# ScalarE's table sets chosen by the functions ahead, and the order of steps replaced, in a two-layer network on one core

## The chip, the cores and the metric

One core of one Trainium2 chip runs the whole kernel. The metric is device microseconds (us) of that core, the median of several runs. The kernel before took 1077.08 us (three runs: 1076.49, 1077.08, 1081.83).

## The reference

The input x is 4 sequences of 1024 rows of 128 values, 4096 rows in fp32. Four residual steps follow each other, each on a layer norm of x:

```python
x = x + attention(layernorm(x))     # 16 heads of width 8, softmax over 1024 keys, inner residual and layer norm
x = x + ffn(layernorm(x))           # silu(x W1) * (x W2), gelu (512x512), gelu (512x512), down to 128
x = x + gla(layernorm(x))           # gated linear attention, 8 heads, a recurrence over 1024 steps per sequence
x = x + zones(layernorm(x))         # per sequence a router picks 3 of 8 experts: gelu_tanh(x Wa) Wb, weighted
```

## The kernel before, in words

The 4096 rows are 8 blocks of 512 (`b` 0 to 7; a sequence is two blocks). The work is cut into 13 streams of steps, each a Python generator in the class `Plan`: `x` attention scores, their exponentials and the weighing of values; `q` the query, key and value projections of the next block; `a` what follows attention; `b` the FFN; `p` projections and decay of the gated linear attention; `r` its replicated value rows (a DMA each); `s` its recurrence, as 128 products, scans and queries; `t` its norm, gate and output, and the router; `w`, `f`, `l`, `z` loads; `d` the experts. The constant `ORDER` is a string of 1805 letters; `Plan.rest` takes the next step of the stream that each letter names. The result is one list of steps (`order`), and each engine's program is that same list, cut down to the steps in which the engine has a part. So the order on every engine and every DMA queue is fixed by that string, each engine works strictly in order, and semaphores are waited on where data come from another engine.

Steps that the text below speaks of:

- `scores` and `weigh` (stream `x`): 256 `scores` steps; in each, TensorE makes two score tiles of 128 x 1024 (4 matmuls, L1448) and ScalarE takes the exponential of both (L914, 512 in all). `weigh`, 512 of them, multiplies an exponentiated tile with the values (L1485). From the seventh of 32 head pairs on, two PSUM areas hold scores, so scores of one step wait for the exponentials of the step before.
- `gate` (L925), `level` with `gelu` (L930), `down`: the FFN of a block. `gate_mm` and `hid_mm` on TensorE are L1517. TensorE works there on a value's high and low part; the low part is made by VectorE (L1222) or, for some, by GpSimd (`parts`, L848).
- `flag` (stream `q`, one per block): GpSimd's PARTITION_ALL_REDUCE (L838), of which block 0's comes at the start. In the order before, block 2's and block 4's stand ahead of a low part of the FFN that TensorE needs next; after, such a part stands just ahead of them. Low parts on GpSimd stand close behind those of blocks 5, 6 and 7 in the order after, queries close behind those of blocks 3 and 4.
- `decay_1`, `decay_3`: Exp (L949), Ln (L951) and Exp (L958). `rms`: Ln (L1003) and then Exp (L1005). `tanh_c` Tanh (L1010), `route_1` Tanh (L1019), `route_2` Exp (L1024).
- `product` and `state` (L1252, L1261) on VectorE and `query` (L862) on GpSimd: the recurrence, 128 times.
- `zone_up` (TensorE L1632, ScalarE L1038) and `zone_down` (TensorE L1644): the experts, 96 each. They start when the last scores are done, since they reuse the attention's memory.

ScalarE's table is loaded by `tables(name)` (L877 to L881; the load itself is an instruction at L881), called ahead of each looked-up function. The rule before: anything with Exp or Ln asks for the set that has both; Gelu and the approximated Gelu ask for a set each; Tanh is content with either Gelu set and else loads the Gelu set. A load is issued only if the set asked for isn't the loaded one. Since the list of steps is known when the program is written, so is each load.

Of the kernel before, what the change touches and what calls it, by code (L numbers as in the profile page):

```python
# [22 lines left out]

ORDER = (
    "xxxxxwxxxxxxqxqxqxxlxxxxxxxxwxxwqxxxxxxxxwxwxxxxxqxxwxxqwxxxfxxxxfxxlxxlxxxxxwxxwxxwxlxwxfxxqfwaxwxx"
    "xxxwxxxxxxxxxwxaawwxxxwaxwwxxqxxwxlafxxxxxxxxxaqxxwxxaxxxwfxbxxwxqbxbbxqbxxfxxbxbbxxxxxlbbxxbqlbbbbb"
    "xbqlxbbbbxbxxxxbfxpxbxbxxppxxxarparxxprpapxxxxxxxssrxasalxraxxxxqxaxxpsssxqbxxsbbxbxxrsqsxxxxsxssssx"
    "xxxxsqxxbsxbbxssbxqxrxxxrxssxlxsxrxsrbssxslxflqsxfsfbbxbxsbbxsbbbsxsfxbrrxxsbrassbbsxsrbxbxsssxaxxsx"
    "axxsxsxssxbrxaxbxaxaxqpxrxpalrxsqpsxsxssrxbxspxppxxqxssssxspxsxsrbxbbbbxxsssfxrxbxrqbxqsxfbxxrsxxbbs"  # L30
    "bssssstbbsxxsbxxxxxxrbrrtsssxxxbbstsllsbxsftblbsrxsxxbxxxbfqsxaxxssxsrsbrxxxxxxxarxxxsfsasxtrxxxsxsx"
    "xxassxsbxslsssxrxpqsrpxxxsqrxsrsxtatpxpsxxxxfaxsxpxxqtqxxxpssasxxspxqxxxxsblqxxtbsbsxbbbtbblrbsrxxxx"
    "xrfstssrslxsxssbsxtstxbbstbbsbbsxbxtbrbrxfrssstxssxbsbsxtasxsbrxbxsassaxxxxxbxsaraxrtsssbxxaxrfsxptp"
    "xsrxsxsxxsxastxsqxbtxqxxtsspsrrqxbsbsxbsxrsxsxxxpxlfrxbqspbpssxsxxpsxbsbxxsxsqxrlssxrqxsbrsxrxxsssxt"
    "xxxxlxxsttlxxsbxfbsxsbbbsbbfxbsrxxtxbbsxrrxsssssrsbssbssssxtratxbsxxbxsxxrsxxssasbaxbxrrlxpxxxxsxxps"
    "txsssxsasaxxfxrtxxsraxsfxrxqxxaxpxqrsbpsxxxsxxtxpxpsxxqssxqbxsxsxqsxxbxlbptxblbbbxssxxrxbxrxslxxstxs"
    "tbssbbsrbsbxsrxtsbsffxssxbxsbtxxrtssrbxsbbssabsrxrxsbsxxbxtxxsxsbtxstxssrxssfsxrxxxaatrxrxsbxppxssxt"
    "xslsxxxsxxassaxxpstsrxxxsrpsxfsxxxrxssrxsxppxasssxtxsaxpxsssxtrxxtrxsrsrsssxbssxtxxxxxtfztsbbfbzbbsb"
    "bdsbdadtssbzbbbsraaddbbbbsdartszdtdsssbsbdarrbsdsssbdabsdssdrdbdadtzbssdrsdrstdddbtdsbddsrddssspssds"
    "zdsrbbtddspsdrdbdrspdsddpbsdbppdsrdbbsssptddbssdssrdrdsbstsbbdsrbdssdssbtsdbrdbstdbssdtsdrsrssrbssbt"  # L40
    "brbssdsssbbtssdtsdbrdrdssrsddbstsssdsrsssdppddstsdrdptdrrsdssdtdsrdddpsspdddtptsststsdpsdssrrssddddd"
    "sdtdsrzsssssdtrsstsdtsrzddsrssdtddsdddsdrssrtsdstsszdsdsrsrsrsssdsrdddddsddsssssdddsrssddtsdddrssddt"
    "ddssdsdtddtddddttddddttddtddtddddtdttdtdtttzdzdddddzdddddddddddddddddddddddddddddddddddddddddddddddd"
    "ddddd"
)

# [427 lines left out]
def build(nc, io, out):  # L474
    ctx = ExitStack()
    with ctx:
# [8 lines left out]
        order = plan.order  # L485
# [386 lines left out]
        def _(act):  # L872
            need = Waits(act, S)
            own = Chain(need, "act")
            loaded = [None]

            def tables(name):  # L877

                if loaded[0] != name:
                    loaded[0] = name  # L880
                    act.preload_act_table_set(name)  # L881

            def log_exp():
# [61 lines left out]

            def decay_1(b):
                own.settle()
                log_exp()
                own.step(act.activation(G2, G2, ACT.Exp, scale=-1.0))  # L949
                own.settle()  # L950
                act.activation(G2, G2, ACT.Ln, bias=1.0).then_inc(S["g_abs"], 1)  # L951

            def decay_3(b):
                need.wait_ge("decayed", 2 * b + 1)
                if b:
                    need.wait_ge("scanned", 16 * b)
                log_exp()
# [74 lines left out]
            def zone_up(b, n, bk, e):  # L1032
                t = 12 * b + n
                need.wait_ge("zone_up_ps", t + 1)
                if t >= NH:
                    need.wait_ge("zone_mm", t - NH + 1)
                tables("gelu_apprx_tanh_and_others")
                act.activation(HH[t % NH], bank(bk), ACT.Gelu_apprx_tanh).then_inc(S["hidden"], 1)  # L1038

            def zone_down(b, m, bk):  # L1040
                if m or b % 2:
                    return
                for n in range(3 * (b // 2), 3 * (b // 2) + 3):
# [662 lines left out]
```

## Time and profile before

| | |
|---|---|
| median of three runs | 1077.08 us (1076.49 to 1081.83) |
| the profiled execution | 1080.35 us, its span 1078.6 us |
| TensorE busy | 978.0 us, 91% |
| ScalarE busy | 846.4 us, 78%; of it 512 exponentials of 128 x 1024 486.8 us, 108 table loads 138.6 us |
| VectorE busy | 707.4 us, 66% |
| GpSimd busy | 343.3 us, 32% |
| mean granted TensorE clock | 0.973 of 2.4 GHz |

The span runs from the first to the last instruction of the core; the 1.75 us between it and the execution's time lie outside. A TensorE matmul's end is modelled, so a busy TensorE need not be at its peak pace. The attention's exponentials run from 26.2 to 794.5 us; what is left of the other streams, and the experts, come after.

### The profile page before, as it was taken

What the parts mean: (1) busy time and instruction counts of PE and PEld (TensorE: products, weight loads), DVE (VectorE), ACT (ScalarE), POOL (GpSimd) and SP (SyncE); (2) the same over time, 40 slices, a digit from 0 to 9 for tenths busy, and PEclk for the clock granted to TensorE, in tenths of its full rate; (3) what the DMA queues carried; (4) which work ended last, traced back from release to release, by engine and by line L of the source; (5) the groups of instructions that cost most, each with busy time, mean ns of one, the idle gap of its engine ahead of it and who ended that gap; (6) DMA issues with size and microseconds to landing.
All of it is one profiled execution on the core that took longest, in us unless ns stands there. A gap on an engine that the chain in (4) does not pass through costs nothing.

```text
span 1078.6 us, 16699 instructions
## 1 busy us (share of the span) xinstructions
PE 978.0 (91%) x5842; PEld 462.2 (43%) x5842; DVE 707.4 (66%) x1267; ACT 846.4 (78%) x1082; POOL 343.3 (32%) x318
## 2 busy tenths in 40 slices
PE   2998989998898799989989999899889999999998
PEld 1222336222442343334423443354237667655666
DVE  4234652565577556878896696778787888989200
ACT  0998996998797799989999989999977377653542
POOL 1000111112442332434522542334332655646100
PEclk8899999899898899999999999999999999999999
DMA  6755352225504361473136431631332321242020
GB/s 165 183 137 126 96 139 57 76 65 131 129 30 126 90 133 57 108 181 95 45 102 162 116 88 61 180 96 55 104 105 73 98 67 62 91 130 83 11 69 20
DMA packets 139975, 106.27 MB, mean 99 GB/s; under 512 B 91824, under 2 KB 106960, under 8 KB 139856
## 3 DMA queue, kind: packets, MB, share of 16 engines
q1 hardware_dynamic: 134960, 102.77, 35.4%
q10 hardware_dynamic: 4896, 1.87, 0.7%
q8 instruction: 79, 1.29, 0.5%
q14 instruction: 40, 0.33, 0.1%
HBM read 75.25 MB, written 29.36 MB: 97 GB/s over the span
## 4 chain that ended last, share of the span: by engine, by line
PE 51%; ACT 17%; issue 14%; DVE 9%; DMA 5%; POOL 4%; SPq 1%; ACTq 0%; DVEq 0%; POOLq 0%
PE PS L1485 15%; ACT R L914 10%; PE PS L1517 9%; PE PS L1448 9%; PE PS L1632 4%; PE PS L1644 4%; DMA R<-VD 3%; DVE R L1252 3%; PE PS L1557 2%; ACT L881 2%; DVE R L1261 2%; PE PS L1579 2%; POOL R L862 2%; PE PS L1588 1%; PE PS L1383 1%
## 5 line engine op out<-in xcount | busy, mean ns | idle before, releaser
L914 ACT ACTIVATE R<-PS 128x1024 f32<-128x1024 f32 x512 | 486.8, 1038 | 52.7 <-PE PS L1448 50.8
L1485 PE MATMUL PS<-R 128*32 128x512 f32 x2048 | 294.0, 617 | 0.2 <-DVE R L1205 0.2
L862 POOL TENSOR_TENSOR R<-R 128x512 f32<-128x512 f32 x128 | 182.2, 1430 | 175.0 <-ACT R L989 121.6
L1448 PE MATMUL PS<-RA 32*128 32x512 f32 x1024 | 189.2, 506 | 46.4 <-ACT R L914 30.5
L1517 PE MATMUL PS<-RB,WR 128*128 128x512 f32 x640 | 183.5, 430 | 24.6 <-DVE R L1228 10.2
L1261 DVE TENSOR_TENSOR_SCAN R<-R 128x512 f32<-128x512 f32 x128 | 192.5, 1504 | 2.9
L1448 PEld LDWEIGHTS PS<-RA 32*128 32x128 f32 x1024 | 73.7, 185 | 273.2 <-ACT R L914 168.6
L881 ACT ACT_TABLE_LOAD x108 | 138.6, 1283 | 48.7 <-PE PS L1517 23.2
L1517 PEld LDWEIGHTS PS<-RB,WR 128*128 128x128 f32 x640 | 121.1, 196 | 86.8 <-issue 22.4
L1252 DVE TENSOR_TENSOR R<-R 128x512 f32<-128x512 f32 x128 | 108.2, 845 | 28.6 <-DMA R<-VD 28.5
L1038 ACT ACTIVATE R<-PS 128x512 f32<-128x512 f32 x96 | 56.6, 596 | 77.1 <-PE PS L1632 76.6
L848 POOL TENSOR_TENSOR RB<-R,RB 128x512 fp32r<-128x512 f32 x48 | 69.6, 1451 | 146.6 <-DVE RB L1217 125.3
L1644 PEld LDWEIGHTS PS<-R 128*128 128x128 f32 x768 | 97.4, 191 | 39.3 <-issue 37.0
L1644 PE MATMUL PS<-R 128*128 128x128 f32 x768 | 100.1, 276 | 2.9 <-ACT R L1047 2.8
L1632 PE MATMUL PS<-XT,R 128*128 128x512 f32 x192 | 99.0, 607 | 2.4 <-DMA R<-in_Wb 2.1
L821 POOL TENSOR_SCALAR rs<-mv 128x4 f32<-128x4 f32 x40 | 15.5, 387 | 248.2 <-DVE mv L1077 230.3
L1485 PEld LDWEIGHTS PS<-R 128*32 128x32 f32 x2048 | 46.9, 109 | 90.7 <-issue 77.4
L1217 DVE CAST RB<-R 128x512 fp32r<-128x512 f32 x64 | 33.9, 530 | 42.2 <-ACT R L930 41.6
L1205 DVE COPY R<-PS 128x512 f32<-128x512 f32 x32 | 22.0, 687 | 59.8 <-PE PS L1485 59.7
L930 ACT ACTIVATE R<-PS,sB 128x512 f32<-128x512 f32 x64 | 42.0, 687 | 11.4 <-PE PS L1517 10.9
L823 POOL TENSOR_TENSOR rs<-rs,half 128x4 f32<-128x4 f32 x40 | 49.1, 1227 | 3.3
L1588 PE MATMUL PS<-R,hot 128*32 128x512 f32 x256 | 42.4, 602 | 5.8 <-POOL R L862 5.1
(123 smaller groups left out, 844.9 us busy)
## 6 DMA issues: line engine op xcount, KB each, us to landing
R<-VD SPq DMA_DIRECT2D x128, 256.0 KB
RA<-QD SPq DMA_DIRECT2D x64, 256.0 KB, 4.5
QD<-RA SPq DMA_DIRECT2D x56, 256.0 KB, 4.0
RA<-QD SPq DMA_DIRECT2D x64, 128.0 KB, 4.4
OD<-R SPq DMA_DIRECT2D x32, 256.0 KB, 2.1
R<-OD SPq DMA_DIRECT2D x128, 32.0 KB, 2.5
R<-in_Wa SPq DMA_DIRECT2D x12, 256.0 KB, 3.3
R<-in_Wb SPq DMA_DIRECT2D x12, 256.0 KB, 3.9
```

Of the source, the lines that this page charges most:

```text
L848: pool.tensor_tensor(part(tile(dst)[:, 1, :]), whole(src), part(tile(dst)[:, 0, :]), ALU.subtract).then_inc(S["lo_pool"], 1)
L862: pool.tensor_tensor(st, st, Qc, ALU.mult).then_inc(S["qh"], 1)
L881: act.preload_act_table_set(name)
L914: act.activation(PR[u % 4], bank(2 * s, 1024), ACT.Exp, scale=SC).then_inc(S["exp"], 1)
L1038: act.activation(HH[t % NH], bank(bk), ACT.Gelu_apprx_tanh).then_inc(S["hidden"], 1)
L1252: dve.tensor_tensor(ST[n % NS], ST[n % NS], Kc, ALU.mult).then_inc(S["kv"], 1)
L1261: dve.tensor_tensor_scan(st, Ac, st, CS[:, v:v + 1] if k else 0.0, ALU.mult, ALU.add).then_inc(S["scanned"], 1)
L1448: op = pe.matmul(bank(2 * s + h), exact(KS[k][p:p + 32, 128 * j:128 * j + 128]), exact(QS[k][p:p + 32, :]), start=True, stop=stop)
L1485: op = pe.matmul(bank(ob)[c:c + 32, :], VAF[b % 2][:, at:at + 32], PR[u % 4][:, 512 * h:512 * h + 512], start=(j == 0), stop=(j == 7), til ...
L1517: return pe.matmul(out_ap, w, x, **kw)
L1632: pe.matmul(bank(bk), WA[r][:, 128 * m:128 * m + 128], xtblock(b), start=True, stop=True).then_inc(S["zone_up_ps"], 1)
L1644: op = pe.matmul(bank(bk)[:, 128 * i:128 * i + 128], HH[t % NH][:, 128 * i:128 * i + 128], WB[r][:, m % 4, :], start=(m == 0 and i == 0), ...
```

## The change

Two things change, nothing else.

1. ScalarE's `tables` takes the function (exp, ln, tanh, gelu, the approximated gelu) and no longer a set. It knows the whole list of functions to come. If the loaded set has the function, nothing is loaded.
2. The string `ORDER` is another one. It has the same letters, each as often, in another order.

```diff
 ORDER = (
-    "xxxxxwxxxxxxqxqxqxxlxxxxxxxxwxxwqxxxxxxxxwxwxxxxxqxxwxxqwxxxfxxxxfxxlxxlxxxxxwxxwxxwxlxwxfxxqfwaxwxx"
+    "qxqxqxxxxxxxxxxxxxwxlxxwxwxxqxwxxxxxxxxxxxwxxxxxxqfxxxxxwxxwxxxlxfxwwxxqxxxxlxqxwxxxxwlxxxxpxfxxxwwf"
...
-            loaded = [None]
-
-            def tables(name):
-
-                if loaded[0] != name:
-                    loaded[0] = name
-                    act.preload_act_table_set(name)
-
-            def log_exp():
-                tables("natural_log_exp_and_others")
-
-            def tanh_with(name):
-                if loaded[0] not in ("gelu_and_others", "gelu_apprx_tanh_and_others"):
-                    tables(name)
+            EXP, LOG, GELU, APPR = "exp_and_others", "natural_log_exp_and_others", "gelu_and_others", "gelu_apprx_tanh_and_others"
+            sets = {"exp": (EXP, LOG), "ln": (LOG,), "tanh": (EXP, GELU, APPR), "gelu": (GELU,), "appr": (APPR,)}
+            uses = {"scores": ("exp",), "gate": ("tanh",), "gelu": ("gelu",), "decay_1": ("exp", "ln"), "decay_3": ("exp",),
+                    "rms": ("ln", "exp"), "tanh_c": ("tanh",), "route_1": ("tanh",), "route_2": ("exp",), "zone_up": ("appr",)}
+            coming = ["exp"] + [f for step in order for f in uses.get(step[0], ())]
+            state = {"loaded": None, "at": 0}
+
+            def tables(function):
+
+                at = state["at"]
+                assert coming[at] == function
+                state["at"] += 1
+                if state["loaded"] not in sets[function]:
+                    def run(name):
+                        return next((n for n in range(at, len(coming)) if name not in sets[coming[n]]), len(coming))
+                    state["loaded"] = max(sets[function], key=run)
+                    act.preload_act_table_set(state["loaded"])
...
             def decay_1(b):
                 own.settle()
-                log_exp()
+                tables("exp")
                 own.step(act.activation(G2, G2, ACT.Exp, scale=-1.0))
                 own.settle()
+                tables("ln")
                 act.activation(G2, G2, ACT.Ln, bias=1.0).then_inc(S["g_abs"], 1)
...
             def rms(b, bk):
                 need.wait_ge("mean_ps", b + 1)
-                log_exp()
+                tables("ln")
                 act.activation(T1, bank(bk), ACT.Ln, scale=1.0 / 16.0, bias=epsc[:, 0:1]).then_inc(S["rms"], 1)
                 need.wait_ge("rms", b + 1)
+                tables("exp")
                 act.activation(T1, T1, ACT.Exp, scale=-0.5).then_inc(S["inv_rms"], 1)
```

The other callers change one word each (`log_exp()` to `tables("exp")`, `tanh_with(...)` to `tables("tanh")`, the two Gelus to `tables("gelu")` and `tables("appr")`).

Walking the list of steps with each rule, as the program text does, gives the loads that are issued (the one at the start included):

| | loads up to the last `scores` step | after it | in all |
|---|---|---|---|
| order before, rule before | 75 | 33 | 108 |
| order after, rule after | 58 | 25 | 83 |

Of the 83, 29 are for Gelu, 11 for the approximated Gelu, 16 bring the set with Ln (8 of them for `rms`, 4 for `decay_1`, 4 for `scores`) and 27 the set with Exp and Tanh. By the same walk the order before with the rule after would issue 87, and the order after with the rule before 140.

Up to head pair 16 (of 32) of the attention the walk counts, without the load at the start, 33 loads before and 23 after.

What lies ahead of the last `scores` step differs by little else: after the change it holds 28 `gate` steps in place of 24 (with the 16 matmuls of L1517 that belong to them), 4 more splittings into parts, one `product` less and one `query` less. The first `hid_mm` of block 6 stands just behind that step. At the very start, the norm of block 1 (`stats`, `apply`) and its four transposes (`turn_in`) now stand around the first `scores` step instead of after the sixth.

## Rows read from the trace of the kernel before

**Rows 1.** The page: busy time, share of the span, instructions of two engines.
```profile
PE 978.0 (91%) x5842; PEld 462.2 (43%) x5842; DVE 707.4 (66%) x1267; ACT 846.4 (78%) x1082; POOL 343.3 (32%) x318
```

**Rows 2.** Busy time by stretch: start:end, length, then each engine.
```profile
26.00:150.00 124.00, 117.36 (x772) 34.13 (x766) 56.01 (x127) 114.19 (x123) 7.31 (x10) 0.96 0.52 131
150.00:415.00 265.00, 237.75 (x1410) 104.99 (x1408) 152.05 (x297) 218.57 (x259) 73.57 (x71) 0.94 0.38 96
415.00:794.50 379.50, 349.63 (x2232) 141.29 (x2230) 298.08 (x526) 355.06 (x449) 145.58 (x132) 1.00 0.39 105
794.50:1078.60 284.10, 265.78 (x1394) 177.53 (x1392) 190.68 (x280) 157.04 (x251) 111.97 (x89) 0.99 0.24 73
```

**Rows 3.** The same stretches for the table loads alone (L881).
```profile
150.00:415.00 265.00, 41.06 (x32) 0.94 0.38 96
415.00:794.50 379.50, 51.32 (x40) 1.00 0.39 105
794.50:1078.60 284.10, 42.34 (x33) 0.99 0.24 73
```

**Rows 4.** Who waited for whom, 415 to 794.5 us: total, times, longest.
```profile
PEld PS L1448 <- ACT R L914: 98.7, 147, 1.7
ACT R L914 <- PE PS L1448: 12.0, 29, 1.8
```

**Rows 5.** The same, 150 to 415 us.
```profile
PEld PS L1448 <- ACT R L914: 58.4, 82, 1.9
ACT R L914 <- PE PS L1448: 16.5, 23, 3.2
ACT L881 <- PE PS L1517: 13.4, 5, 5.5
PE PS L1517 <- POOL RB L848: 7.8, 4, 4.4
```

**Rows 6.** Groups of instructions by line, the whole span.
```profile
L914 ACT ACTIVATE R<-PS 128x1024 f32<-128x1024 f32 x512 | 486.8, 1038 | 52.7 <-PE PS L1448 50.8
L881 ACT ACT_TABLE_LOAD x108 | 138.6, 1283 | 48.7 <-PE PS L1517 23.2 <-issue 11.6 <-PE PS L1632 5.8
L925 ACT ACTIVATE R<-PS,sB 128x512 f32<-128x512 f32 x32 | 21.7, 686 | 15.5 <-PE PS L1517 15.3
```

**Rows 7.** ScalarE in order of time: start, length, instruction.
```profile
400.56 1.94 ACT L914 ACTIVATE R<-PS 128x1024 f32<-128x1024 f32 x2
402.52 1.28 ACT L881 ACT_TABLE_LOAD   x1
403.82 0.60 ACT L1010 ACTIVATE R<-PS 128x512 f32<-128x512 f32 x1
...
524.06 3.77 ACT L914 ACTIVATE R<-PS 128x1024 f32<-128x1024 f32 x4 [0.48 <-PE PS L1448]
```

**Rows 8.** The start, in order of time.
```profile
7.59 1.11 PE L1369 MATMUL PS<-ident,R 128*128 128x128 f32 x4 [7.59 <-DVE R L1086]
...
26.19 3.77 ACT L914 ACTIVATE R<-PS 128x1024 f32<-128x1024 f32 x4 [13.05 <-PE PS L1448]
26.45 1.12 DVE L1086 TENSOR_SCALAR R<-X,mv,rs 128x128 f32<-128x128 f32 x4 [5.80 <-POOL rs L823]
```

**Rows 9.** Around two of GpSimd's reductions, in order of time.
```profile
173.26 2.50 POOL L848 TENSOR_TENSOR RB<-R,RB 128x512 fp32r<-128x512 f32 x2 [7.30 <-issue]
...
365.26 0.37 POOL L838 PARTITION_ALL_REDUCE R<-R  x1 [5.92 <-issue]
...
372.60 1.25 POOL L848 TENSOR_TENSOR RB<-R,RB 128x512 fp32r<-128x512 f32 x1 [6.97 <-issue]
...
373.90 5.70 PE L1517 MATMUL PS<-RB,WR 128*128 128x512 f32 x17 [4.38 <-POOL RB L848]
374.72 1.28 ACT L881 ACT_TABLE_LOAD   x1 [5.46 <-PE PS L1517]
```

**Rows 10.** The chain of waits that ended last, 794.5 to 1078.6 us, by line.
```profile
by line: PE PS L1632 14.7%; PE PS L1644 14.4%; DMA R<-VD 12.9%; DVE R L1252 8.4%; DVE R L1261 7.9%; issue 7.7%; POOL R L862 4.3%; PE PS L1517 3.9%; PE PS L1588 2.6%; DMA R<-in_Wb 1.7%; ACT L881 1.7%; PE PS L1557 1.3%; POOL rs L823 1.1%; SPq
```

More of the change, by code:

```diff
@@ L31 @@
[L31 to L40, printed above, removed]
@@ L41 @@
[L41 to L43 removed]
+    "qxqxqxxxxxxxxxxxxxwxlxxwxwxxqxwxxxxxxxxxxxwxxxxxxqfxxxxxwxxwxxxlxfxwwxxqxxxxlxqxwxxxxwlxxxxpxfxxxwwf"
+    "wxxwxxaxxxwxwxxaawxxxawaqxxwxlxxxxaxxxxxqxwxawxfxxbwxxxxxwxqxxxbxxbbxxbbxbqxxxbbxlqxxbxxbbbbbbxblxxb"
@@ new lines @@
+    "xxlfbfbbxxbxxxqfxxxbxxxxxaaxbxxabxxaxplpxxrrrxpqaqpxpxapqqxfxpxaxxsxxxxbxsxbxsxxsqsxxsxssrxxxssbxqxx"
+    "rxxxlssxbxrssfxbxfbxlxssssbrxxbbrsxxsxxxlxxsxsrxsrsbsxbxbbbfbbxbxssxabssbxssrsrssbsrsbsxxrbbxxsaasxs"
+    "xbxxxsbaxxpssxpsxaxqrsxsrasxxxqssrlxfppxrabqxxxpsxpxsssxspxxxbxsssxxxxxbrqxxrbxbxbxrbxbxbssqsxstxbts"
+    "rbstssxsxbsbsqbbbxxssxxxxrsbststlxrxxfrbllxbbrssxbssxssfsbxsbxxfaxxxxbssrxaaxxrsrxxsxssxxxsrbsxaxpsx"
+    "xpssxxsssxqasxrrxxxxsxsxqxrsprsaqxtxlxtxspxxaxqxpsxbpsxssxspsxxbxxxftqssxbxbrbrrxxbxxxxxqsblsslrxxbb"
@@ new lines @@
+    "sxxlstfsxxsbssxtssbsbsrbxfbbbtxbssxrxbbsxfssbsrsaxbssarssstxbxaxbtxaxtxxxxsbrxxatrxxsxxxtsxsbasrxxsx"
+    "fsssasxtrspxqslxxbpssrxrxrqbqspxqtxxbstbxpsxsqsbxtxxxxsxppttssxsrxxlbxpxssxssxxbxrbsxrrxrsssxxsxslxs"
+    "sxtsssttbxxsfsrlxxtxfxsfsqbbbbbtxbxrbxsxbssxtbsbrxsbssbxxxtarssbxbxaxxasxxasbrraslxxaxrsxxxxsbxsssxs"
+    "qpsxxpsxrxxtxspxsqasxsprxxxbsxsxxrsxrfrssxsqxpxpxsxfqsxsxpxxstbsxxsxsxtxqbrlxbxxbxbrbxsxrbxrlsxlxbtx"
+    "sssxssbssbxfxbbbbbfbssxxxstsxbrxrtxarsssxbssrsbssstsbxbxxbtxxxabxssasxrtrxbxrsssrxsppsxxsxsxxsxxasxx"
@@ new lines @@
+    "xxpxxsstsftsrpaxxxxsssxrxarssxxtsrxapbpsssxsltxpxxxfsbsxsxtrbbbrxxbrxsbrxsbssxtxxsfxbxxtxxtsssbxszbf"
+    "btbbtstsbssbdrbadtbbabassbdazzasbbdatrrsdsddtdsdsrdtddbadbbssssdsdsrbprstdsdbddsdrdbpdsddbdddrzdtsbs"
+    "dszsdsbtsbdsbzdsdpsprtdsdsdrbsssrpbspdssrsdbsbpsbssrbsbddbtrsssdrdddsrdsdssstssdtsbsrttrbsdrssssbdbr"
+    "ssdsdsbddbsttsssdbdrdrssdsbrdrsstsssdppsddpsssdsddprdstrddddtdssstdspdrstrdtddpsstssdsptssrsrdddtdss"
+    "srdsddztsrsssddtsdtssdzstrsssrsdddrddsrtsdsssddtsdsdssrsrszssdrdsrdsddsddsdtdsssdsddsddrssdsdrdssdsd"
@@ L44 @@
+    "dsdtdsdtddtdddtdtddtddttdddddtdddtdttdtttzztdzdddddddddddddddddddddddddddddddddddddddddddddddddddddd"
     "ddddd"
@@ L923, in gate @@
                     need.wait_ge(*free)
-                tanh_with("gelu_and_others")
+                tables("tanh")
                 act.activation(HL[0][m][:, 1, :], bank(ba), ACT.Tanh, scale=sB[:, m:m + 1]).then_inc(S["tanh"], 1)
@@ L928, in gelu @@
                 need.wait_ge(*ps)
-                tables("gelu_and_others")
+                tables("gelu")
                 act.activation(HL[L][m][:, 1, :], bank(bk), ACT.Gelu, scale=sB[:, scale + m:scale + m + 1]).then_inc(S["gelu"], 1)
@@ L947, in decay_1 @@
                 own.settle()
-                log_exp()
+                tables("exp")
                 own.step(act.activation(G2, G2, ACT.Exp, scale=-1.0))
                 own.settle()
+                tables("ln")
                 act.activation(G2, G2, ACT.Ln, bias=1.0).then_inc(S["g_abs"], 1)
@@ L956, in decay_3 @@
                     need.wait_ge("scanned", 16 * b)
-                log_exp()
+                tables("exp")
                 act.activation(Ac, G1, ACT.Exp, scale=1.0 / 16.0).then_inc(S["decayed"], 1)
@@ L1001, in rms @@
                 need.wait_ge("mean_ps", b + 1)
-                log_exp()
+                tables("ln")
                 act.activation(T1, bank(bk), ACT.Ln, scale=1.0 / 16.0, bias=epsc[:, 0:1]).then_inc(S["rms"], 1)
                 need.wait_ge("rms", b + 1)
+                tables("exp")
                 act.activation(T1, T1, ACT.Exp, scale=-0.5).then_inc(S["inv_rms"], 1)
@@ L1008, in tanh_c @@
                 need.wait_ge(*ps)
-                tanh_with("gelu_and_others")
+                tables("tanh")
                 act.activation(Z1, bank(bk), ACT.Tanh, scale=0.5).then_inc(S["tanh_c"], 1)
@@ L1017, in route_1 @@
                 need.wait_ge("route_ps", 2 * bt + 1)
-                tanh_with("gelu_and_others")
+                tables("tanh")
                 act.activation(router[0:32, bt, 2:3], bank(bk)[0:32, 0:1], ACT.Tanh, bias=b1r[:, 0:1]).then_inc(S["route_act"], 1)
@@ L1022, in route_2 @@
                 need.wait_ge("logits_r", bt + 1)
-                log_exp()
+                tables("exp")
                 act.activation(router[:, bt, 16:24], router[:, bt, 8:16], ACT.Exp).then_inc(S["route_act"], 1)
@@ L1036, in zone_up @@
                     need.wait_ge("zone_mm", t - NH + 1)
-                tables("gelu_apprx_tanh_and_others")
+                tables("appr")
                 act.activation(HH[t % NH], bank(bk), ACT.Gelu_apprx_tanh).then_inc(S["hidden"], 1)
```

4 lines of the change are left out of this document (removed).

## The prediction

> **What bounds the kernel now.** I read the page's first part, then busy time by stretch, then the chain and the waits. The page puts TensorE first, 91%, and ScalarE at 78% [rows 1]. That average hides two stages. Up to 794.5 us the 512 exponentials run, and there ScalarE is busy 92% (26 to 150), 82% (150 to 415) and 94% of the stretch (355.06 of 379.50); behind them it falls to 55%, with TensorE at 94% [rows 2]. TensorE's 92% in the third stretch is pipelined matmuls with modelled ends, so busy time doesn't say who sets the pace; the waits do. From 415 to 794.5 us TensorE's weight loads of the scores wait 98.7 us in 147 places for an exponential, while ScalarE waits 12.0 us for scores [rows 4]. So there **ScalarE sets the pace**. Between 150 and 415 us it is less plain: ScalarE has 46 us idle in 265 [rows 2], waiting 16.5 us for scores and 13.4 us, in 5 places of up to 5.5 us, for the FFN's products, some of these held up by GpSimd (7.8 us) [rows 5]; the granted clock is 0.94 against 1.00 later [rows 2], nearer the upper of its two levels (2.4 GHz, the other 1.2) in both.
>
> After 794.5 us the chain is mixed: the experts' two matmul lines 29%, the recurrence (replica DMA, product, scan, query) 12.9 + 8.4 + 7.9 + 4.3 = 33.5%, table loads 1.7% [rows 10].
>
> **The change, part by part.** The profiled execution took 1080.35 us with a span of 1078.6, 3.3 us above the median of 1077.08; I sum differences and take them from the median.
>
> *Table loads ahead of the last scores: 75 become 58, 17 fewer.* The walk gives 75 before, and the trace has 33 of 108 behind 794.5 us [rows 3], so the walk and the trace agree. A load lasts 1283 ns, each one [rows 6]. What it takes from ScalarE is a little more. Two exponentials start at 400.56 and last 1.94, the load starts at 402.52, the next activation at 403.82 [rows 7]: gaps of 0.02 and 0.02 us. Without a load two activations overlap: four exponentials take 3.77 us, 0.94 each, against 1.94/2 = 0.97 in a group of two [rows 7] and 1.04 for one [rows 6], so neighbours overlap by some 0.1 us, which a load between them forbids. 0.02 + 1.28 + 0.02 + 0.08 = **1.40 us a load**. 17 x 1.40 = **-23.8 us**, on the path where ScalarE sets the pace. Ten of the 17 fall before pair 16 (up to about 400 us), where it is the pace only in part; I let them count in full, because there too TensorE's weight loads wait for exponentials in 82 places, 58.4 us, more than three times what ScalarE waits for scores [rows 5], and keep 10 x 1.40 = 14 us for the range.
>
> The Trainium skill, "ScalarE: Activation LUTs", section What ACT_TABLE_LOAD costs, puts a drain of about 1.38 us on top of the 1283 ns, 2.66 us for a switch; this trace agrees with the 1283 and shows no such gap on either side [rows 7]; by the page 17 loads would be 45 us. The same page's rules for kernel authors speak against splitting Exp and Ln over sets (the joint set is one load, not two). Here the new rule does pay for it.
>
> Ln now forces a load where Exp's set is in: 8 loads for `rms` and 4 for `decay_1` among the 83. They are in the counts already, so no term of their own. They stand in chains with little behind them at once; if one lands on the path, 1.40 us.
>
> *Table loads behind the last scores: 33 become 25, 8 fewer.* ScalarE is busy 157 of 284 us [rows 2], so TensorE's work and the recurrence cover them: **0**. With the cover gone, -8 x 1.40 = -11 us; that end goes into the range.
>
> *Work pulled ahead of the last scores.* Four `gate` steps more: 4 x 0.686 [rows 6] = **+2.7 us** on ScalarE. Sixteen matmuls of L1517 leave the tail. The nearest row has 17 in 5.70 us [rows 9], 0.34 each, so up to 5.4 us of TensorE. A third of the tail's chain is the recurrence [rows 10], which gets one product more, so I take **-3** of the bounds 0 and -5.4.
>
> *The start.* The four transposes of block 1 now stand on TensorE between the first and second `scores`, and wait for a norm that ends at 26.45 + 1.12 = 27.57 us; transposes at the cold start took 1.11 us [rows 8]. So the second scores start at about 28.7 and their first exponential at about 29.5, where before four exponentials ran on from 26.19 [rows 8], the third at 28.1: **+1.5 us**, between 0 and +3.
>
> *GpSimd's reductions.* Behind each of the eight PARTITION_ALL_REDUCE GpSimd stands still for 7.0 to 7.3 us [rows 9]. Before, one of them falls between the gates' third and fourth low part, so that TensorE waits 4.38 us and ScalarE 5.46 us for it [rows 9]. In the new order the block's fourth low part stands ahead of the reduction at both such places (blocks 2 and 4), but pooled parts follow others closely. I take half of the 4.4: **-2 us**, bounds -8 (all of the 7.8 us [rows 5]) and +8 (the same again somewhere else).
>
> *The rest of the order.* The same instructions and DMAs on each queue, in another order; SP's queue carries the same transfers. Nothing in the trace prices the new interleaving: bounds -8 and +8, from the 7.8 us that TensorE waits for one kind of GpSimd's work [rows 5], taken at 0.
>
> Sum: -23.8 + 2.7 - 3 + 1.5 - 2 = **-24.6 us**, so 1077.1 - 24.6 = **1052.5 us**.
>
> **The rivals.**
>
> *Rival 1, TensorE keeps the pace.* If up to 415 us the freed ScalarE time only becomes idle time, 14 us come back: 1066.5. If that holds later as well, nothing is left but small terms: 1077. For it: TensorE's 91%, and its 90% against ScalarE's 82% from 150 to 415 [rows 2]. Against: the 98.7 us of waits on the exponentials [rows 4]. Chance 0.17, half of it above 1071.7.
>
> *Rival 2, slower, a GpSimd hole behind the reductions.* The new order puts a pooled low part within one or two scores steps behind the reduction in blocks 5, 6 and 7, and queries behind those of blocks 3 and 4. If TensorE, which works in order, reaches the consumer within the 7.2 us, the scores behind it wait too and ScalarE runs dry. Seven reductions at 7.2 us are 50; less the 7.8 us paid before [rows 5] that is +43, and with -22.6 from the other terms +20: 1097. It decides from an average stall of (22.6 + 7.8)/7 = 4.3 us a reduction. Against: between such a part and its consumer lie mostly other gates and scores. Chance 0.06.
>
> *Rival 3, a load costs its surroundings too.* ScalarE idled 48.7 us just before the 108 loads [rows 6], 0.45 each. If that goes with the load, and the tail counts: 25 x (1.28 + 0.45) = 43.3, with the other terms' -0.8 that is 1033. By the Trainium skill's 2.66 us (the same page and section) the 25 would be an estimated 66.5 us, 1010. Against both: 11.6 of the 48.7 is the start, and most of the rest waits for products that come no sooner. Chance 0.05.
>
> *Rival 4, the change doesn't do what it says.* If the set with Exp doesn't serve Tanh, and loads are put in after all, the new order comes near its 140 loads under the old rule: 32 x 1.40 = +45, 1122. Chance 0.02.
>
> **How the numbers follow.** Forecast 0.70, rivals 0.17, 0.06, 0.05, 0.02. 0.5%, about what a measurement of this kernel can tell from no change, is 5.4 us: faster means below 1071.7. Faster: 0.68 of the forecast, 0.09 of rival 1, 0.05 of rival 3: 0.82. Same: 0.02 of the forecast's own upper end and 0.08 of rival 1: 0.10. Slower: rivals 2 and 4, 0.08. The forecast's own range: down to 1040 with the tail's loads or the stalls gone, up to 1066 with rival 1's 14 us. To hold 8 in 10 it reaches on to 1074, through most of rival 1.
>
> **What would show it.** Right: 83 loads, 58 before the last exponential; ScalarE's busy time down by 25 x 1.28 = 32 us to about 814; the exponentials' end, 794.5 now, at about 794.5 - 23.8 + 2.7 + 1.5 - 2 = 773; the tail 281 us instead of 284 [rows 2]; the second pair of exponentials about 1.5 us later. Wrong: as many loads gone but ScalarE's idle time before 415 us grown by 10 us or more (rival 1); TensorE waiting on L848 or L862 by over 20 us (rival 2); the last exponential before 755 (rival 3); more than 83 loads (rival 4). The forecast fails as a whole if the stretch up to the last exponential shrinks by less than 12 us.

## The result, and the profile after

The changed kernel takes 1045.09 us (four runs, 1042.45 to 1051.1) against 1077.63 us for the kernel before, a ratio of 0.970 with a 95% interval of 0.965 to 0.975: **32.5 us faster**. The forecast was 1052.5 us, 24.6 us faster, in a range of 1040 to 1074. The profiled execution took 1046.05 us, its span 1044.2.

The page's busy times:

```profile
PE 962.5 (92%) x5842; PEld 454.1 (43%) x5842; DVE 720.2 (69%) x1267; ACT 813.4 (78%) x1057; POOL 359.4 (34%) x318
```

Busy time by stretch (start:end, length, then TensorE, its weight loads, VectorE, ScalarE, GpSimd, granted clock, DMA share, GB/s); the last exponential ends at 772.9 us here:

```profile
26.00:150.00 124.00, 120.62 (x833) 37.57 (x830) 61.96 (x142) 116.03 (x126) 10.62 (x13) 0.97 0.54 137
150.00:415.00 265.00, 242.56 (x1487) 102.69 (x1485) 166.42 (x312) 226.07 (x273) 79.52 (x74) 0.96 0.38 99
415.00:773.00 358.00, 335.27 (x2116) 136.68 (x2112) 297.42 (x508) 325.17 (x418) 156.88 (x131) 0.99 0.41 107
773.00:1044.20 271.20, 256.54 (x1374) 173.16 (x1372) 183.95 (x268) 144.56 (x239) 107.37 (x85) 0.99 0.25 76
```

They answer to [rows 2]. ScalarE's busy time is 813.4 us, where 814 was foretold, and the exponentials end at 772.9, where 773 was. The tail behind them is 271.3 us against 284.1 and against 281 in the forecast. So the sum missed in the tail, by 10 us, and seems to have hit the attention's part to a tenth. The experiments show that this second hit was luck in good part: taken apart in the kernel before, neither of its two large terms is what the sum had.

The table loads by stretch (they answer to [rows 3]): 83 in all, 25 behind the exponentials.

```profile
150.00:415.00 265.00, 33.36 (x26) 0.96 0.38 99
415.00:773.00 358.00, 39.77 (x31) 0.99 0.41 107
773.00:1044.20 271.20, 32.08 (x25) 0.99 0.25 76
```

Who waited for whom in the changed kernel (total, times, longest), TensorE from 26 to 772.9 us, and below it ScalarE:

```profile
PE PS L1453 <- ACT R L917: 17.3, 52, 0.7
PE PS L1593 <- POOL R L862: 7.5, 4, 4.4
PE PS L1522 <- POOL RB L848: 5.0, 2, 4.0
...
ACT R L917 <- PE PS L1453: 62.3, 64, 13.1
ACT L891 <- PE PS L1522: 9.6, 5, 5.4
ACT R L968 <- POOL R L862: 5.2, 1, 5.2
```

L1453, L1522, L1593 and L917 are L1448, L1517, L1588 and L914 of before. Against the kernel before, over the same part, TensorE waits less for exponentials and less for low parts:

```profile
PE PS L1448 <- ACT R L914: 30.5, 79, 2.1
...
PE PS L1517 <- POOL RB L848: 9.6, 6, 4.4
```

but a wait for GpSimd's queries (L862), which wasn't there over this part, has come in. It is looked at below.

### The profile page after: what moved, and what is told of

Read it like the earlier page. It is cut to its first block, busy times and chain, and to the rows that moved or that the text cites. A ratio compares the mean times of both kernels' runs of the same rounds, so it can differ in the third digit from the quotient of the medians.

```text
span 1044.2 us, 16674 instructions
## 1 busy us (share of the span) xinstructions
PE 962.5 (92%) x5842; PEld 454.1 (43%) x5842; DVE 720.2 (69%) x1267; ACT 813.4 (78%) x1057; POOL 359.4 (34%) x318
## 4 chain that ended last, share of the span: by engine, by line
PE 56%; issue 14%; ACT 12%; DVE 10%; POOL 4%; DMA 3%; SPq 0%; DVEq 0%; ACTq 0%; POOLq 0%
PE PS L1490 17%; PE PS L1453 10%; PE PS L1522 9%; ACT R L917 8%; PE PS L1649 5%; PE PS L1637 5%; DVE R L1266 3%; PE PS L1562 3%; PE PS L1584 2%; DMA R<-VD 2%; DVE R L1257 2%; POOL R L862 2%; PE PS L1593 2%; PE PS L1388 1%; ACT L891 1%
## 5 line engine op out<-in xcount | busy, mean ns | idle before, releaser
L917 ACT ACTIVATE R<-PS 128x1024 f32<-128x1024 f32 x512 | 489.0, 1037 | 65.4 <-PE PS L1453 62.3
L862 POOL TENSOR_TENSOR R<-R 128x512 f32<-128x512 f32 x128 | 196.3, 1542 | 180.1 <-ACT R L993 108.2
L1453 PE MATMUL PS<-RA 32*128 32x512 f32 x1024 | 176.8, 501 | 34.1 <-ACT R L917 17.3
L1266 DVE TENSOR_TENSOR_SCAN R<-R 128x512 f32<-128x512 f32 x128 | 199.8, 1561 | 3.2
L1522 PE MATMUL PS<-RB,WR 128*128 128x512 f32 x640 | 177.8, 420 | 12.0 <-POOL RB L848 5.0
L1453 PEld LDWEIGHTS PS<-RA 32*128 32x128 f32 x1024 | 68.6, 183 | 251.6 <-ACT R L917 154.7
L1522 PEld LDWEIGHTS PS<-RB,WR 128*128 128x128 f32 x640 | 117.7, 192 | 80.3 <-issue 35.3
L1257 DVE TENSOR_TENSOR R<-R 128x512 f32<-128x512 f32 x128 | 112.3, 878 | 35.1 <-DMA R<-VD 33.9
L1649 PEld LDWEIGHTS PS<-R 128*128 128x128 f32 x768 | 98.7, 193 | 39.1 <-issue 38.0
L1490 PEld LDWEIGHTS PS<-R 128*32 128x32 f32 x2048 | 46.9, 109 | 95.4 <-issue 82.2
L1593 PE MATMUL PS<-R,hot 128*32 128x512 f32 x256 | 49.3, 616 | 10.7 <-POOL R L862 10.7
L823 POOL TENSOR_TENSOR rs<-rs,half 128x4 f32<-128x4 f32 x40 | 46.5, 1162 | 3.3
L1343 DVE TENSOR_TENSOR X<-PS,X 128x512 f32<-128x512 f32 x8 | 5.5, 685 | 52.4 <-PE PS L1649 52.4
```

The lines of the kernel that those rows point to most:

```text
L862: pool.tensor_tensor(st, st, Qc, ALU.mult).then_inc(S["qh"], 1)
L1257: dve.tensor_tensor(ST[n % NS], ST[n % NS], Kc, ALU.mult).then_inc(S["kv"], 1)
L1266: dve.tensor_tensor_scan(st, Ac, st, CS[:, v:v + 1] if k else 0.0, ALU.mult, ALU.add).then_inc(S["scanned"], 1)
L1453: op = pe.matmul(bank(2 * s + h), exact(KS[k][p:p + 32, 128 * j:128 * j + 128]), exact(QS[k][p:p + 32, :]), start=True, stop=stop)
L1490: op = pe.matmul(bank(ob)[c:c + 32, :], VAF[b % 2][:, at:at + 32], PR[u % 4][:, 512 * h:512 * h + 512], start=(j == 0), stop=(j == 7), til ...
L1522: return pe.matmul(out_ap, w, x, **kw)
```

## The experiments

All ratios are to the kernel before, timed on the same chip. "Attention" is from the first exponential to the end of the last, "tail" from there to the end of the span, both in the profiled execution. Single executions scatter: three that run the same instructions (changed, e3_tail2, e4_att2) have attentions of 746.7, 751.0 and 745.7 us and tails of 271.3, 272.1 and 270.6. The profiled execution of before lies 3 us above its median, that of e2_order 4 us below.

| run | loads | attention, us | tail, us | median, us | ratio (95%) |
|---|---|---|---|---|---|
| before | 108 | 768.3 | 284.1 | 1077.6 | 1 |
| changed | 83 | 746.7 | 271.3 | 1045.1 | 0.970 (0.965 to 0.975) |
| e1_rule | 87 | 761.5 | 284.4 | 1073.6 | 0.996 (0.993 to 0.999) |
| e2_order | 140 | 815.7 | 272.9 | 1120.9 | 1.043 (1.037 to 1.049) |
| e5_more | 146 | 811.2 | 282.2 | 1122.7 | 1.045 (1.039 to 1.051) |
| e6_tail20 | 103 | 749.5 | 278.1 | 1053.4 | 0.978 (0.972 to 0.985) |
| e7_new40 | 40 | 745.9 | 268.6 | 1043.1 | 0.970 (0.964 to 0.977) |
| e8_early_zone | 84 | 747.3 | 283.2 | 1058.4 | 0.986 (0.979 to 0.993) |
| e9_old40 | 40 | 767.4 | 283.4 | 1082.8 | 1.006 (1.003 to 1.008) |
| e10_old_nored | 87 | 755.7 | 276.9 | 1062.9 | 0.987 (0.982 to 0.992) |
| e11_new_nored | 83 | 720.8 | 271.6 | 1023.1 | 0.950 (0.947 to 0.953) |
| e12_banks | 83 | 746.8 | 270.2 | 1044.8 | 0.970 (0.965 to 0.976) |

### e1_rule and e2_order: the change cut in two

e1_rule is the changed kernel with the old string, e2_order the kernel before with the new one:

```diff
 ORDER = (
-    "qxqxqxxxxxxxxxxxxxwxlxxwxwxxqxwxxxx...
+    "xxxxxwxxxxxxqxqxqxxlxxxxxxxxwxxwqxxx...
```

> The rule of the change with the order of before: 87 loads, 55 up to the last scores (20 fewer than before) and 32 behind it (1 fewer). Theory A (a load costs 1.40 us up to the last scores and nothing behind it, as the prediction has it): 1077.6 - 20 x 1.40 = about 1050 us, the exponentials end at 794.5 - 28 = 766, the tail stays at 284. Theory B (a load costs as much behind the last scores): 1048, not to be told from A here. Theory C (the tail's 12.8 us in the changed kernel came from the new order): the tail keeps its 284 us here, and the order is worth what is left, some 5 us. Rival (TensorE sets the pace up to 415 us, so that only the loads after that pay): some 1063.

> The order of the change with the rule of before: 140 loads, 115 up to the last scores (57 more than the changed kernel) and 25 behind it (as many). Theory A: 1045.1 + 57 x 1.40 = 1125 us, all of it before the exponentials' end, the tail 271 us as in the changed kernel. If only the loads where ScalarE sets the pace count, half of that: about 1085.

The rule alone makes the kernel 0.4% faster, not 2.6%. Twenty loads fewer shorten the attention by 6.8 us, 0.34 us a load in place of 1.40. That is little more than single executions scatter, but the interval of the ratio, 0.993 to 0.999, is far from theory A's 2.6%. The order alone makes the kernel 4.3% slower, 1120.9 us where theory A had 1125: by this run alone theory A would have stood. The two together are worth far more than their sum. The stretch from 26 us to the end of the exponentials, for before, e1_rule, the changed kernel and e2_order, in that order:

```profile
26.00:794.50 768.50, 704.74 (x4410) 280.42 (x4404) 506.14 (x949) 687.82 (x829) 226.46 (x212) 0.97 0.40 106
```
```profile
26.00:787.60 761.60, 698.63 (x4410) 277.36 (x4404) 501.12 (x947) 662.45 (x809) 227.20 (x212) 0.97 0.40 107
```
```profile
26.00:772.90 746.90, 698.36 (x4429) 276.90 (x4426) 525.70 (x961) 667.27 (x815) 246.91 (x217) 0.98 0.42 109
```
```profile
26.00:842.00 816.00, 732.97 (x4423) 283.40 (x4420) 523.28 (x962) 744.41 (x872) 239.48 (x217) 0.93 0.38 100
```

In e1_rule ScalarE works 25.4 us less than before (687.82 - 662.45) and the stretch is 6.9 us shorter: 18.5 us turned into idle time, and TensorE idles 63.0 us against 63.8. That is the mechanism of rival 1, though the new order hid it. The step from e1_rule to the changed kernel has TensorE as busy (698.4) and ScalarE a little busier, and is 14.7 us shorter: it is TensorE's idle time that fell, from 63.0 to 48.5 us. In e2_order the 57 loads more than in the changed kernel cost 69.0 us of attention, 1.21 us each (75.8 us of the whole by the medians, 1.33 each); ScalarE is busy 91% of it. Part of that price is TensorE's own: its granted clock is 0.93 there against 0.98 and its busy time 34.6 us longer.

How the attention's gain splits therefore depends on which half comes first: with the rule first it is 6.8 us and then 14.8 for the order; with the order first it is 47.4 us lost and then 69.0 won. The run that would tell most, the new order with 75 loads up to the last scores like the kernel before, wasn't made. On a straight line between the changed kernel and e2_order it would lie an estimated 17 x 1.21 = 20.6 us above the changed kernel, within 1 us of the kernel before. So it isn't shown that the new interleaving is faster at an equal number of loads; what is shown is that with 58 or fewer of them it is.

The tail is plainer: 284.4 us with the old order and the new rule, 272.9 with the new order and the old rule. The tail's 12.8 us come from the order, theory C; the order by itself also takes the tail's loads from 33 to 25 (the trace of e2_order has 25 there).

### e5_more, e7_new40 and e9_old40: loads put in and taken out

e5_more is the kernel before with 38 loads put in:

```diff
                 if loaded[0] != name:
                     loaded[0] = name
+                    if name == "gelu_and_others" and state["early"]:
+                        act.preload_act_table_set("gelu_apprx_tanh_and_others")
                     act.preload_act_table_set(name)
```

> The kernel before with 38 loads more up to the last scores: each load of the Gelu set there is preceded by one of the other Gelu set (146 in all). Theory D (new: an order of steps hides little of a load that it wasn't made for, and gives little back for one that is taken out of it, 0.34 us each in the order before): 38 x 1.3 = 49 us slower than before, 1129. If loads in the order before are mostly covered anyway (the 0.34 us of the rule alone holds both ways): 13 us, 1093.

e7_new40 is the changed kernel with Tanh in place of the FFN's 64 exact Gelus, so that part of the computation is left out and another of the same cost stands there; e9_old40 is the same with the old order:

```diff
-                tables("gelu")
-                act.activation(HL[L][m][:, 1, :], bank(bk), ACT.Gelu, scale=sB[:, scale + m:scale + m + 1]).then_inc(S["gelu"], 1)
+                tables("tanh")
+                act.activation(HL[L][m][:, 1, :], bank(bk), ACT.Tanh, scale=sB[:, scale + m:scale + m + 1]).then_inc(S["gelu"], 1)
```

> The changed kernel with Tanh computed in place of the FFN's 64 exact Gelus (same cost of an activation, so 40 loads in all: 21 up to the last scores in place of 58, 19 behind). Theory A (each load pays 1.3 to 1.4 us wherever ScalarE sets the pace): 1045 - 37 x 1.35 = 995 us. Theory D (taken out of an order that was made with them, they give about 0.34 us each): 1045 - 13 = 1032 us, and ScalarE's idle time up to the exponentials' end grows from 80 to about 115 us.

> The order of before with the new rule and with Tanh computed in place of the FFN's 64 exact Gelus (40 loads, 21 up to the last scores, 19 behind). Theory E (new: TensorE with its fixed interleaving sets the pace once ScalarE is relieved, and the new order lowers that floor): the exponentials end near 787, as with 55 loads, and the time is within 4 us of the 1073.6 of the rule alone, some 28 us above the changed kernel although it has 43 loads fewer. Theory A (loads pay wherever they are taken out): 1073.6 - 34 x 1.35 = 1028 us.

Each load put into the old order costs 1.13 us of attention (42.9 us over 38), 1.25 of the whole by the medians of the runs made together (1122.7 - 1075.2 = 47.5 over 38). But taking 37 out of the attention's part of the changed kernel gives 0.8 us there, 0.02 us a load and less than the scatter, and taking 54 of 75 out of the old order's gives 0.9 us, less than taking 20 out had. The rows of e7_new40, same columns as above, and of its loads:

```profile
26.00:772.20 746.20, 699.82 (x4429) 277.26 (x4426) 527.29 (x961) 620.31 (x778) 246.64 (x217) 0.97 0.42 109
```
```profile
L891 ACT ACT_TABLE_LOAD x40 | 51.3, 1283 | 24.2 <-issue 11.6 <-DVE R L1266 8.0 <-PE PS L1601 2.7
```

ScalarE works 47.0 us less than in the changed kernel (667.27 - 620.31), and the stretch is 0.7 us shorter. TensorE's busy time is the same to 1.5 us, and its waits for exponentials stay too (16.0 us in 50 places, in the changed kernel 17.3 in 52). **Once ScalarE isn't overloaded, its work doesn't set the pace any more; the order of the steps does.** That the pace is then TensorE's, with what it waits for in that order, is argued from its 94% busy and not shown; GpSimd's share in it follows below. The two orders have different floors: 761 to 767 us of attention for the old one with 55 or 21 loads up to the last scores, 746 for the new one with 58 or 21. With its 75 the kernel before stood 1 to 7 us above its floor; the new order's 58 stand on it. So the price of a load is not one number but has a kink: 1.1 to 1.3 us above what the order has room for, nearly nothing below. Theory A is out. Theory D had the price of a load put in (1129 us, 1122.7 measured) but not of one taken out (1032, 1043.1 measured), and theory E holds in kind, though e9_old40 took 1082.8 us where it had 1073.6 within 4.

e9_old40 is even 0.9% slower than e1_rule (intervals 1.003 to 1.008 and 0.993 to 0.999), with 47 loads fewer. TensorE is 5.2 us longer busy and idle 1 us longer there, at a clock of 0.96 against 0.97 (behind 415 us 0.96 against 0.99); the cause stays open.

### e3_tail2 and e4_att2: loads issued twice

Both put a second `act.preload_act_table_set(state["loaded"])` behind the first, e3_tail2 behind the last scores, e4_att2 up to them.

> The changed kernel with each of the 25 loads behind the last scores issued twice. Theory A (covered): within 3 us of 1045. Theory B (the tail's loads are on the path, so that 8 fewer gave 11 of the 12.8 us): 1045 + 25 x 1.3 = 1078 us. In between, the cost per load times 8 is what the loads gave the tail.

> The changed kernel with each of the 58 loads up to the last scores issued twice (the first one stands in ScalarE's idle start, 57 count). Theory A: a second load adds 1.30 us (1.28 and a gap of 0.02; the overlap was lost to the first): 57 x 1.30 = 74, so 1119 us. Rival (TensorE or bubbles cover part of them): 1080 to 1100, with ScalarE's idle time before the exponentials' end falling from about 57 us.

Neither tells anything: the second load of a set that is in was dropped, and the trace of each has 83 loads. So they are two more measurements of the changed kernel: 1046.29 us (0.970) and 1043.21 us (0.969). e5_more and e6_tail20 therefore put in loads of another set.

### e6_tail20: do the tail's loads count?

```diff
+                own_sets = sets if at <= 366 else {"exp": (LOG,), "ln": (LOG,), "tanh": (EXP,), "gelu": (GELU,), "appr": (APPR,)}
-                if state["loaded"] not in sets[function]:
+                if state["loaded"] not in own_sets[function]:
```

> The changed kernel with 20 more loads behind the last scores (45 in place of 25; Exp and Ln only from their joint set, Tanh only from Exp's set there), 103 in all. Theory A (covered there): within 3 us of 1045, the tail 271. Theory B (on the path): 20 x 1.3 = 26 us, 1071. The 8 fewer loads of the change gave the tail 8/20 of what this costs.

Between the two theories: 20 loads make the tail 6.8 us longer, 278.1 against 271.3, 0.34 us each, and the whole by the medians 8.3 us, 0.42 each. By that the 8 that went were worth an estimated 3 us where the prediction had 0.

### e8_early_zone: the tail's opening

The letters of the changed order behind the last scores; three steps of the experts move ahead of the FFN's:

```diff
-    szbfbtbbtstsbssbdrbadtbbabassbdazz...
+    szdddbfbtbbtstsbssbrbatbbabassbazz...
```

> The changed kernel with the first three experts' up products put right behind the load of their weights, ahead of the FFN's products of block 6 (84 loads). Theory C (of the tail's 12.8 us, the opening gave 7 to 8: before, TensorE stood 4.4 us in the first 15.5 us and fell to the lower clock for some of it, waiting for gates and for the weights' DMA): TensorE waits about 4 us for the DMA here, and the tail grows by 3 to 6 us, 1049. If the opening doesn't matter because the recurrence sets the tail's length: within 2 us of 1045.

The tail grows by 11.9 us, to 283.2, twice to four times what I expected, and within 1 us of the old order's tail. TensorE in order of time behind the last scores, first e8_early_zone, then the changed kernel:

```profile
773.88 1.06 PE L1490 MATMUL PS<-R 128*32 128x512 f32 x8
781.45 5.49 PE L1637 MATMUL PS<-XT,R 128*128 128x512 f32 x6 [6.50 <-DMA R<-in_Wb]
785.95 4.25 PE L1522 MATMUL PS<-RB,WR 128*128 128x512 f32 x13
```
```profile
774.29 3.99 PE L1522 MATMUL PS<-RB,WR 128*128 128x512 f32 x16
778.22 1.07 PE L1593 MATMUL PS<-R,hot 128*32 128x512 f32 x8
779.21 2.13 PE L1522 MATMUL PS<-RB,WR 128*128 128x512 f32 x8
781.25 1.95 PE L1637 MATMUL PS<-XT,R 128*128 128x512 f32 x4
```

The experts' weights can't be loaded before the attention is done, since they take its memory. In e8_early_zone TensorE has them 6.5 us behind the last weighing of values, at 781.45 us. The changed order has 7 us of FFN and recurrence products to put on TensorE in that time; with the experts put first it stands 6.50 us, then runs at the lower clock, six matmuls in 5.49 us where four took 1.95. In the first 25.5 us of the tail it gets through 56 matmuls (by the record), in the changed kernel through 133. The first 15.5 us of the tail in the kernel before, in two stretches, whose order came to the experts after four gates:

```profile
794.50:800.00 5.50, 3.53 (x15) 1.68 (x13) 4.52 (x11) 3.56 (x5) 0.00 (x0) 1.00 0.21 66
800.00:810.00 10.00, 7.70 (x14) 3.62 (x15) 9.59 (x12) 3.74 (x5) 7.50 (x6) 0.69 0.59 169
```

There it is 4.3 us idle and the granted clock 0.69 for 10 us; in the changed kernel's first 10 us TensorE is busy throughout, at 1.00:

```profile
773.00:783.00 10.00, 10.00 (x46) 5.53 (x45) 9.62 (x16) 5.62 (x8) 3.33 (x3) 1.00 0.34 100
```

How much of the old opening is the clock, a later run tells in part. e10_old_nored has the old order and the 32 tail loads of e1_rule, TensorE idles 3.5 us in the same two stretches, but the clock stays at 1.00, and its tail takes 276.9 us, 7.5 less than e1_rule's. The second stretch there:

```profile
787.90:797.90 10.00, 8.10 (x25) 4.15 (x24) 9.59 (x11) 5.67 (x8) 7.58 (x6) 1.00 0.61 171
```

The clock is not all of it: e9_old40 and e5_more, at 0.83 there, have tails of 283.4 and 282.2 us. No run has the clock as its only difference.

### e10_old_nored, e11_new_nored and e12_banks: GpSimd's reductions

The reduction of the eight `flag` steps goes to TensorE, which turns each column of 128 maxima into a row, and VectorE, which takes the row's maximum; e11_new_nored has the new order, e10_old_nored the old one, both the new rule:

```diff
-            self.add("flag", b)
+            self.add("flag", b, self.take("a"))
...
-                pool.partition_all_reduce(am[:, 16 + 2 * b:18 + 2 * b], am[:, 2 * b:2 * b + 2], 128,
-                                          io["rmax"]).then_inc(S["amax_all"], 1)
+                for c in range(2):
+                    op = pe.matmul(bank(bk)[0:1, 128 * c:128 * c + 128], am[:, 2 * b + c:2 * b + c + 1], ident[:, :],
+                                   start=True, stop=True)
+                op.then_inc(S["amax_all"], 1)
...
+                dve.tensor_reduce(am[0:1, 16 + 2 * b:18 + 2 * b],
+                                  bank(bk)[0:1, 0:256].rearrange("p (i q) -> p i q", i=2), AX.X,
+                                  ALU.max).then_inc(S["amax_row"], 1)
```

e12_banks keeps the reduction and changes only the turn of the PSUM banks that came with it:

```diff
+            self.take("a")
             self.add("flag", b)
```

> The order of before with the new rule, and GpSimd's eight reductions of the largest query and key values replaced: TensorE turns the column into a row (two matmuls of 128 columns), VectorE takes the row's maximum. GpSimd is then never out for 7 us before and after them. Theory F (what the new order mends in the attention's part are the holes behind the reductions, where TensorE waited 12.7 us for low parts): 10 to 14 us faster than the rule alone, 1060 to 1064. If the holes were a small part of it: 1069 to 1074.

> The changed kernel with the same replacement of GpSimd's reductions. TensorE waits 5.0 us for low parts and 7.5 us for queries there, ScalarE once 5.2 us for a query, and the start's stall of 1.3 us comes from the norm that stands behind a reduction on GpSimd. Theory F: 6 to 12 us faster than the changed kernel, 1033 to 1039. If other waits take their place: within 3 us of 1045.

> The changed kernel with GpSimd's reductions kept, and only the other thing changed that came with their replacement: each flag step of blocks 1 to 7 takes a PSUM bank out of turn, so that later steps use other banks. If the 22 us that the replacement gave come from GpSimd's holes: 1045 within 3 us, the exponentials' end at 773. If they come from the turn of the banks: 1023, the end at 748.

Without the reductions the changed kernel takes **1023.1 us**, 22 us less and 5.0% below the kernel before, the fastest of all, where I expected 6 to 12 us less. The banks alone give nothing (0.970), and TensorE's waits for GpSimd in the attention fall from 12.5 us to 1.8, so it is GpSimd's holes. In the old order they were worth 10.7 us (1073.6 to 1062.9), as theory F had it, but of these only 5.8 lie in the attention (761.5 to 755.7); the rest is in the tail, where no reduction stands and where the clock didn't fall this time. In the new order the attention gains 25.9 us (746.7 to 720.8) and the tail nothing. That turns theory F round: the new order doesn't mend the holes, it suffers more from them, 2.0% of the time against 0.9%, each to about 0.6%. One of them in the changed kernel, behind block 4's reduction, GpSimd, TensorE and ScalarE in order of time:

```profile
352.47 0.37 POOL L838 PARTITION_ALL_REDUCE R<-R  x1 [6.08 <-issue]
360.44 4.26 POOL L862 TENSOR_TENSOR R<-R 128x512 f32<-128x512 f32 x3 [7.61 <-issue]
...
362.12 3.70 PE L1593 MATMUL PS<-R,hot 128*32 128x512 f32 x5 [4.44 <-POOL R L862]
...
368.26 3.77 ACT L917 ACTIVATE R<-PS 128x1024 f32<-128x1024 f32 x4 [7.92 <-PE PS L1453]
```

GpSimd stands 7.61 us behind the reduction, three queries are late, TensorE waits 4.44 us for them with the scores behind in its queue, and ScalarE has nothing for 7.92 us. In e11_new_nored the attention's row is

```profile
26.00:747.70 721.70, 687.51 (x4457) 276.61 (x4458) 529.40 (x964) 667.31 (x815) 243.56 (x209) 0.99 0.43 113
```

TensorE is idle 34.2 us in place of 48.5, and its busy time, at a clock of 0.99 in place of 0.98, is 10.9 us shorter, with 28 more matmuls in the record.

## Why the prediction was right, and where it wasn't

The verdict and the range were right, and the size was 8 us short. By its steps:

- **"17 x 1.40 = -23.8 us, on the path where ScalarE sets the pace": failed for the kernel that it was read from.** ScalarE doesn't set the pace there in the sense the step needs. The rule alone takes 20 loads out and gives 6.8 us; 37 more out of the new order give 0.8. The 98.7 us of weight loads waiting for exponentials [rows 4] don't show that ScalarE is the bound. Weight loads are short, and their row counts the time from one to the next as idle, so that it shows more than the matmul waits (7.41 us against 6.50 for the one wait of e8_early_zone); the matmuls' own waits for exponentials were 30.5 us in 79 places over the whole attention, and even such waits aren't there to be won, since 16.0 of 17.3 us stayed in e7_new40. Rival 1 had its mechanism right for the rule by itself, with 1066 to 1077 us against the 1073.6 measured, and was discounted for the wrong row. With the rule taken first, the attention's 21.6 us are 6.8 of the rule and 14.8 of the new order, whose interleaving I had taken at 0 with bounds of 8 and whose other terms there at +2.2 (2.7 + 1.5 - 2). Against the sum's -23.8 and +2.2 these are two errors of 17 us that cancelled, which is luck. With the order first, the estimate above (20.6 us for 17 loads, the interleaving near nothing) would agree with the sum, but no run shows it, and nothing in the rows of before said that the new order would make the loads count.
- **1.40 us for a load** is a little high as the price of one too many: 1.13 us (e5_more) and 1.21 (e2_order) of attention, 1.25 and 1.33 of the whole by the medians. The 2.66 us of the Trainium skill ("ScalarE: Activation LUTs", What ACT_TABLE_LOAD costs) is not borne out: 57 and 38 loads more cost about half of that each. The same page's rule (Rules for kernel authors), that Exp and Ln belong into one set, spoke against the change; for the order before, the new rule has 87 loads all the same where the old one has 108.
- **The tail's loads at 0: an estimated 3 us**, by 0.34 to 0.42 us each, inside the bound of 11.
- **The work pulled ahead, -3 in the tail: the term was mis-sized, with the opening left out.** The tail lost 12.8 us. e8_early_zone shows that an opening with the wrong work over the weights' transfer can by itself cost 12, though it stands 6.5 us where the old order's stood 4.3; e10_old_nored's tail, 7.5 us shorter with the old order, bears the opening's clock out as a large part. How the 12.8 divide between opening, loads and work pulled ahead isn't shown. The trace of before had the sign: its clock falls to 0.69 just behind 800 us.
- **The start, +1.5 us: 1.32 measured.** The changed kernel's row, which answers to [rows 8], has the second pair of exponentials wait for it:

```profile
26.36 1.11 DVE L1091 TENSOR_SCALAR R<-X,mv,rs 128x128 f32<-128x128 f32 x4 [7.20 <-POOL rs L823]
27.53 1.12 PE L1374 MATMUL PS<-ident,R 128*128 128x128 f32 x4 [1.49 <-DVE R L1091]
...
29.42 1.94 ACT L917 ACTIVATE R<-PS 128x1024 f32<-128x1024 f32 x2 [1.32 <-PE PS L1453]
```

- **GpSimd's reductions, -2 us: the wrong sign.** At block 4, where the step counted on a gain because the low part now stands ahead of the reduction, the queries behind it took its place (the 4.44 and 7.92 us above). Rival 2 had named the mechanism and these queries. Its price was about four times too high: the holes cost the changed kernel 22 us and the old order 11, so the change made them 11 us dearer, where the rival had 43 more. The premise for both was too plain as well: not behind each of the eight does GpSimd stand for 7.0 to 7.3 us. Before, block 0's is followed at once by the next instruction, and block 6's by 10.4 us.
- **Rival 4's price:** 32 loads on the path, 1122 us, where by the sum's own count 40 more lie up to the last scores and 8 fewer behind. By that count it would have been 40 x 1.40 = 56 us more, 1133. e2_order, which has those 140 loads, took 1120.9.
- Of the signs that were to show the forecast right, 83 loads, ScalarE's 814 us and the end of the exponentials at 773 all came out, and were no proof. The one that could tell, ScalarE's idle time before 415 us growing by 10 us or more in rival 1, can't be read from the changed kernel, since the order changed with the rule: there it fell from 56.2 to 46.9 us (26 to 415 us). Even in e1_rule, with the rule alone, it grew only to 61.5, so the sign was set too high to tell.

Left open is what in the new interleaving lowers the floor by 15 us, or by 35 us with GpSimd's holes gone in both (755.7 against 720.8). The waits point to a spreading out (TensorE waits for exponentials 17.3 us against 27.3 in e1_rule, for low parts 5.0 against 12.7), but no run moves one of them alone. How much of the changed kernel's gain an order made for the old rule could have had wasn't tried either.

## What to carry to other kernels

In this program, whose order is fixed, two busy engines stood near a balance, and the price of work on one of them had a kink: what was added cost nearly in full, what was taken out gave little. Expect the same where you see such a balance. Don't cost a removal by the time that weight loads wait, and take the matmuls' own waits for no more than an upper bound (17.3 us of them, and 37 loads out gave 0.8). Measure the parts of a change apart before you believe a sum that fits. Look at where a stage opens on a transfer that couldn't start earlier, and have as much ready work lie over it as it takes.

## What was not expected of the hardware

- A GpSimd PARTITION_ALL_REDUCE of 0.37 us (a rough figure, as spans on GpSimd are) takes the engine away for far longer: for blocks 2 to 7, in both kernels, GpSimd is idle 6 to 9 us ahead of it, and behind it 6.9 to 7.6 in nine cases of twelve and up to 10.8 in the others. The eight cost the changed kernel 22 us; two matmuls of 128 columns and a VectorE maximum do what is needed of them with no such hole.
- A 6.5 us wait of TensorE for a transfer went with 12 us in the end. Behind it the clock fell: over these 16 us of e8_early_zone it is 0.68 of 2.4 GHz (a mixture of its two levels):

```profile
772.00:788.00 16.00, 9.50 (x27) 4.62 (x27) 5.44 (x11) 6.40 (x8) 1.87 (x2) 0.68 0.18 57
```

- With loads added to ScalarE, TensorE's granted clock was lower over the attention: 0.97 before and 0.95 in e5_more, 0.98 in the changed kernel and 0.93 in e2_order.
